# A step-by-step order written by hand: early products at steps of their own, a reordered front, and contexts divided two pairs at a time

## The chip, the cores and the metric

The kernel runs on one core of a Trainium2 chip. The metric is device microseconds for one execution, lower is better. TensorE (PE, with its weight loads as PEld) multiplies, VectorE (DVE), ScalarE (ACT) and GpSimd (POOL) do elementwise work, and SyncE (SP) starts most DMAs. Every engine runs its own instructions strictly in the order in which they were written for it, and semaphores order the engines among each other.

## The reference, cut to what matters

One transformer layer in float32 over x of 8 batches x 256 tokens x 256 features.

```
h = layernorm(x)
q, k, v = h @ Wq, h @ Wk, h @ Wv         # 32 query heads, 8 key heads, head size 8
q, k = rope(q), rope(k)
p = softmax(causal(q k^T / sqrt(8)))      # four query heads share a key head
x = x + layernorm((p v) @ Wo + b_out)
x = x + layernorm(moe(layernorm(x)))      # router top 2 of 8 experts, and 2 shared ones
```

The change touches only the attention part; the experts' part that follows is the same code.

## The kernel before

**The unit of work.** Attention is cut into 64 units, one for each batch and key head; unit k belongs to batch k // 8. A unit has four query heads of 256 tokens. For it the kernel needs the row maxima of the scores first, with queries along the partitions: `early(k)` makes the products of the first 128 tokens (one PSUM bank), `late(k)` those of the last 128 tokens (two neighbouring banks). On VectorE `tops(k)` (line 1069) takes the maxima of the first and `lates(k)` (line 1073) those of the second. After four units GpSimd makes three bf16 parts of the negated maxima (`neg`), TensorE turns them (`turn`), ScalarE copies them out (`turned`), and SP's DMA writes them into the query tile. `pass2(n)` makes the scores again, now with keys along the partitions and the maxima already subtracted, `exp` (line 922) takes the exponential, GpSimd zeroes what is not causal (line 1491), and `weigh(n)` multiplies with the values and a column of ones into bank 7, two units (a pair) side by side. `weighed` copies a pair's sums into `YC` (two buffers), `back` turns them to tokens along the partitions, and `divide` (lines 1082 and 1085) takes the reciprocal of the sums and multiplies the contexts into `CTX`, two buffers of one batch each. `b_turn`, `b_out` and so on carry a batch half (a tile of 128 tokens) through the output projection, layernorms and router.

**The order.** `plan()` writes one list of stages, and each engine walks it and takes its own stages. The list goes by steps n from -24. In step n the stages `early`, `tops`, `late`, `lates` of unit n + 7 stand beside `pass2(n)` and `exp(n)`; `weigh(n - 2)` follows. The string `ORDER` gives the order within a step; its s0 to s3 are quarter steps, at which the parts of the front (`FRONT0` for batch 0, `FRONT1` for batch 1, `FRONT` for the rest) and of the back (`BACK`) stand at slot 32 * batch + offset, and the second tile a lag later. In the front, `f_stats` and `f_dev` take a tile's statistics, `f_qkv` makes its products, `f_taken` (ScalarE) scales them out, `f_rope`, `f_first` to `f_fourth` (VectorE) and `k_first`, `k_third`, `k_twice` (ScalarE) turn them to rope and to three bf16 parts, and `q` and `k` are the DMA transposes on SP's queue into `QT` and `KT`. After the second tile's `k`, SP loads x of the batch two further on.

**Banks.** `banks()` gives each product of this part the least recently taken of PSUM banks 3 to 6. A product waits until the reader of the bank's last content has freed it: `divide` frees the bank of a `back`, `lates` that of a `late`, `b_low` that of a `b_turn2`, and so on.

**Idle products.** `WARM` lists how many products of a constant tile `mean` TensorE makes, with no reader, behind a stage, one number for each index: 12 ahead of the product that centres the weights (`mean`), 34 behind `f_qkv(3)`, and 14, 5, 4, 3, 3, 3, 3 behind `early(0)` to `early(6)`, 6 behind `late(0)`.

Of the kernel before, what the change touches and what calls it, by code (L numbers as in the profile page):

```python
# [5 lines left out]
F32 = mybir.dt.float32  # L6
# [3 lines left out]
ALU = mybir.AluOpType  # L10
# [3 lines left out]
P = 128  # L14
# [14 lines left out]
for k in range(NK):  # L29
# [6 lines left out]
EPS = 1e-5  # L36
LEAD = 7
START = -24
LAGS = (8, 12)
LAG = 16  # L40
EARLY = 55
SOON = 16
SHARED = 8
SPLIT = 6
WARM = {"mean": (12,), "f_qkv": (0, 0, 0, 34), "early": (14, 5, 4, 3, 3, 3, 3), "late": (6,)}
JOIN = 64
LAST4 = NT - 4
# [12 lines left out]


PICKS = ((0, 14), (14, 2))
# [62 lines left out]
def plan():  # L125

    out = []
    ahead = {}
    for n in range(64):
        ahead.setdefault(n - min(LEAD, LEAD + n // 2), []).append(n)  # L130
    halves, turns, turned, pairs, divided = [], [], [], [], []

    def sides(n):
        for b in range(NB):
            for stages, lag in (((FRONT0, FRONT1)[b] if b < 2 else FRONT, LAGS[b] if b < 2 else LAG), (BACK, 16)):
                for what, at in stages.items():
                    for T in range(2):
                        if n == max(32 * b + at + lag * T, 4 * START):
                            out.append((what, 2 * b + T))
                            if out[-1] == ("f_dev", 1):  # L140
                                out.append(("mean", 0))

    def step(n):
        firsts = ahead.get(n, [])
        for o in ORDER.split():
            if o == "2" and 0 <= n < 64:
                out.append(("pass2", n))
            if o == "x" and 0 <= n < 64:
                out.append(("exp", n))
            if o == "a":  # L150
                out.extend(("early", k) for k in firsts)
            if o == "d":
                out.extend(("tops", k) for k in firsts)
            if o == "b":
                out.extend(("late", k) for k in firsts)
            if o == "l":
                out.extend(("lates", k) for k in firsts)
            if o == "w" and 0 <= n - 2 < 64:
                out.append(("weigh", n - 2))
            if o == "W" and 0 <= n - 2 < 64 and n % 2:  # L160
                out.append(("weighed", (n - 2) // 2))
                pairs.append((n - 2) // 2)
            if o == "v":
                out.extend(("back", k) for k in pairs)
                divided.extend(pairs)
                pairs.clear()
            if o == "V":
                out.extend(("divide", k) for k in divided)
                divided.clear()
            if o == "m0":  # L170
                for k in firsts:
                    if k % 4 == 3:
                        out.append(("neg", k // 4, 0))
                        halves.append([k // 4, 1])
            if o in ("m1", "m2", "m3"):
                for h in halves[:1]:
                    if h[1] == int(o[1]):
                        out.append(("neg", h[0], h[1]))
                        h[1] += 1
                        if h[1] == 4:  # L180
                            turns.append(halves.pop(0)[0])
            if o == "t":
                out.extend(("turn", m) for m in turns)
                turned.extend(turns)
                turns.clear()
            if o == "T":
                out.extend(("turned", m) for m in turned)
                turned.clear()
            if o[0] == "s":
                sides(4 * n + int(o[1]))  # L190
# [10 lines left out]
    for c in range(NC + 4):  # L201
# [40 lines left out]
        if LAST + 4 <= c < LAST + 2 + NT:  # L242
            m = c - LAST - 2
# [71 lines left out]
def build(nc, x, xt, wqkv, wo, bout, wr, wsh, wa, wb, wc, rope, cf32, cbf, crf, out):  # L315
    ctx = ExitStack()
    with ctx:
# [3 lines left out]
        def sb(name, shape, dt, stack=ctx):  # L321
            return stack.enter_context(nc.sbuf_tensor(name, shape, dt))
# [3 lines left out]
        def bank(b, lo=0, hi=512):  # L326
            return PS[:, 512 * b + lo:512 * b + hi]
# [14 lines left out]
        identf = CF[:, 0:128]  # L342
# [11 lines left out]
        WRX = sb("WRX", [P, 2, 2, 8], F32R)  # L354

        behind = ExitStack()
        CTX = sb("CTX", [P, 2, 2, 256], F32, behind)
# [11 lines left out]
        sb("rest", [P, 320], F32)  # L369

        att = ExitStack()

        def ab(name, shape, dt):
            return sb(name, shape, dt, att)
# [5 lines left out]
        mean = ab("mean", [P, P], F32)  # L380
# [9 lines left out]
        RC = ab("RC", [P, 2, 8], F32)  # L390
# [7 lines left out]
        XTX = ab("XTX", [P, 2, 2, 2, 128], F32R)  # L398
        ident = CB[:, 0:128]
        corner = CB[:, 128:160]  # L400
        att.close()

        WH = [sb("WH0", [P, 3840], F32R)]
# [6 lines left out]
        early = ExitStack()  # L410
# [5 lines left out]
        late = ExitStack()  # L416
# [35 lines left out]
        full = [sem(f"full{b}") for b in range(8)]  # L452
        free = [sem(f"free{b}") for b in range(8)]
# [26 lines left out]
        right0, top0, laid, n_m, scored, expd, pv, sums, zeroed, ev = (sem(n) for n in ("right0", "top0", "laid", "n_m", "scored", "expd", "pv", "sums", "zeroed", "ev"))  # L480
# [4 lines left out]
        stages = plan()  # L485
# [63 lines left out]
        def _(eng):  # L549
            e = Waits(eng)  # L550
# [218 lines left out]
            for s in stages:  # L769
                what, i = s[0], s[1]  # L770
                if what == "mean":
# [3 lines left out]
                    c = take(s)  # L775
                    for k in range(2):
                        t = mm(bank(c, 0, 384), mean[:, :], WQ[:, k, :], k == 0, k == 1)
                    t.then_inc(full[c], 1)
                elif what == "f_qkv":
# [3 lines left out]
                    c = take(s)  # L783
# [17 lines left out]
                elif what == "turn":  # L801
                    e.wait_ge(n_3, i + 1)
                    c = take(s)
                    o = bank(c, 0, 128).bitcast(BF16)
# [5 lines left out]
                elif what == "weigh":  # L810
                    weigh(i)
                elif what == "back":
                    e.wait_ge(ev, i + 1)
                    e.wait_ge(d_cf, 16)
                    half_turn(s, YC[:, i % 2, :], identf)
                elif what == "b_turn":
                    for k in range(4):
                        read(e, ("back", 4 * (i // 2) + k))
                    half_turn(s, CTX[:, i // 2 % 2, i % 2, :], identf)
# [44 lines left out]
        def _(eng):  # L864
# [9 lines left out]
            for s in stages:  # L874
# [48 lines left out]
                elif what == "weighed":  # L923
                    h = i
                    e.wait_ge(pv, 2 * h + 2)
                    made(e, ("back", h - 2))
# [78 lines left out]
        def _(eng):  # L1005
# [68 lines left out]
                                      AXX, ALU.max, negate=True).then_inc(n_m, 1)  # L1074

            def divide(k):
                b, a = k // 4, k % 4
                c = use["back", k][0]
                src = bank(c, 0, 256).rearrange("p (t h x) -> p t h x", t=2, x=16)
# [632 lines left out]
```

## Time and profile before

| | us |
|---|---|
| median of three runs (657.97 to 658.33) | 658.25 |
| the profiled execution | 659.02 |
| its span, first to last instruction | 657.1 |

Read it so: the span is the part of an execution that the trace shows; 1.9 us lie around it. The first 45 us are the front before `exp(0)`, the steps of attention run from 45 to about 245 us, and from about 250 us on TensorE works on the experts' part. In the trace a product with float32 operands has two records, so that 12 idle products are 24 records.

### The profile page before, as it was taken

What the parts mean: (1) busy time and instruction counts of PE and PEld (TensorE: products, weight loads), DVE (VectorE), ACT (ScalarE), POOL (GpSimd) and SP (SyncE); (2) the same over time, 40 slices, a digit from 0 to 9 for tenths busy, and PEclk for the clock granted to TensorE, in tenths of its full rate; (3) what the DMA queues carried; (4) which work ended last, traced back from release to release, by engine and by line L of the source; (5) the groups of instructions that cost most, each with busy time, mean ns of one, the idle gap of its engine ahead of it and who ended that gap; (6) DMA issues with size and microseconds to landing.
All of it is one profiled execution on the core that took longest, in us unless ns stands there. A gap on an engine that the chain in (4) does not pass through costs nothing.

```text
span 657.1 us, 15356 instructions
## 1 busy us (share of the span) xinstructions
PE 631.5 (96%) x5934; PEld 518.5 (79%) x5934; DVE 531.3 (81%) x1055; ACT 423.2 (64%) x798; POOL 333.6 (51%) x528
## 2 busy tenths in 40 slices
PE   8997899999999979999999999999999999999995
PEld 6854456666655547888899999999999999888884
DVE  5699999999998744479879888888988888558886
ACT  2437788889887875542257876787877787422222
POOL 3227667877766761100275454545454530078864
PEclk9998999999999999999999999999999999999998
DMA  3953633655540000000367786877776864032311
GB/s 91 177 128 77 107 84 70 131 111 145 112 88 12 19 10 17 17 1 1 120 234 257 248 279 212 266 245 255 242 265 234 260 220 153 25 91 83 94 56 64
DMA packets 79671, 87.10 MB, mean 133 GB/s; under 512 B 54352, under 2 KB 69072, under 8 KB 79600
## 3 DMA queue, kind: packets, MB, share of 16 engines
q0 software_dynamic: 11872, 54.53, 25.1%
q1 hardware_dynamic: 67312, 31.08, 19.3%
q8 instruction: 47, 0.77, 0.5%
q10 hardware_dynamic: 416, 0.52, 0.3%
q14 instruction: 24, 0.20, 0.1%
HBM read 63.83 MB, written 9.31 MB: 111 GB/s over the span
## 4 chain that ended last, share of the span: by engine, by line
PE 79%; DVE 12%; issue 3%; ACT 3%; POOL 2%; SPq 1%; DMA 1%; POOLq 0%; DVEq 0%; ACTq 0%
PE PS L553 75%; DVE NM L1073 3%; DVE NM L1069 2%; PE PS L564 2%; PE PS L760 1%; ACT PF L922 1%; POOL PF L1491 1%; DVE X L1338 1%; DVE RR L1034 1%; PE PS L708 1%; DMA X<-in_x 1%; DVE RA L1027 1%; ACT WH L869 0%; POOL RS L1434 0%; SPq L1593 0%
## 5 line engine op out<-in xcount | busy, mean ns | idle before, releaser
L1278 DVE TENSOR_TENSOR HF<-SS,PS 128x256 f32<-128x256 f32 (+2 forms) x141 | 68.6, 487 | 66.7 <-ACT SS L968 37.9
L1357 DVE TENSOR_TENSOR WL<-RAW,WH 128x768 fp32r<-128x768 f32 x125 | 118.4, 958 | 4.4 <-ACT WH L869 4.1
L968 ACT ACTIVATE SS<-PS 128x256 f32<-128x256 f32 (+2 forms) x141 | 62.0, 440 | 79.2 <-PE PS L553 77.5
L869 ACT ACTIVATE HH<-HF 128x256 fp32r<-128x256 f32 (+1 forms) x120 | 58.0, 483 | 72.6 <-DVE HF L1278 70.3
L1491 POOL TENSOR_SCALAR_AFFINE_SELECT PF<-PF 128x512 f32<-128x512 f32 x128 | 83.1, 674 | 41.5 <-ACT PF L922 41.3
L869 ACT ACTIVATE WH<-RAW 128x768 fp32r<-128x768 f32 x125 | 103.3, 841 | 0.0
L553 PE MATMUL PS<-WH,HH 128*128 128x256 f32 x355 | 103.2, 291 | 0.2
L553 PE MATMUL PS<-WL,HH 128*128 128x256 f32 x355 | 100.3, 282 | 0.0
L553 PE MATMUL PS<-WH,HL 128*128 128x256 f32 x355 | 100.2, 282 | 0.0
L922 ACT ACTIVATE PF<-PS 128x1536 f32<-128x1536 f32 x64 | 92.8, 1449 | 11.4 <-PE PS L553 10.1
L553 PE MATMUL PS<-XGL,WH 128*128 128x256 f32 x320 | 90.5, 283 | 0.0
L553 PE MATMUL PS<-XGH,WH 128*128 128x256 f32 x320 | 90.3, 282 | 0.0
L553 PE MATMUL PS<-XGH,WL 128*128 128x256 f32 x320 | 90.3, 282 | 0.0
L1073 DVE TENSOR_REDUCE NM<-PS 128x4 f32<-128x1024 f32 x64 | 77.6, 1213 | 1.0 <-PE PS L553 0.9
L553 PEld LDWEIGHTS PS<-WH,HH 128*128 128x128 f32 x355 | 67.5, 190 | 2.7 <-ACT HH L869 0.3
L553 PEld LDWEIGHTS PS<-WL,HH 128*128 128x128 f32 x355 | 67.5, 190 | 2.0
L553 PEld LDWEIGHTS PS<-WH,HL 128*128 128x128 f32 x355 | 67.7, 191 | 0.0
L553 PE MATMUL PS<-XH,WH 128*128 128x512 f32 x160 | 64.1, 401 | 0.0
L1463 POOL DMA_INDIRECT RAW<-in_wa,WIDX x23 | 22.7, 985 | 80.5 <-DVE WIDX L1248 40.3
L553 PE MATMUL PS<-XL,WH 128*128 128x512 f32 x160 | 63.4, 396 | 0.0
L553 PE MATMUL PS<-XH,WL 128*128 128x512 f32 x160 | 63.1, 394 | 0.0
L1371 DVE TENSOR_TENSOR HL<-HF,HH 128x256 fp32r<-128x256 f32 (+1 forms) x120 | 62.3, 519 | 0.2 <-ACT HH L869 0.2
(212 smaller groups left out, 1488.3 us busy)
## 6 DMA issues: line engine op xcount, KB each, us to landing
ys<-YO SPq DMA_DIRECT2D x16, 256.0 KB, 3.1
RAW<-in_wsh SPq DMA_DIRECT2D x4, 768.0 KB, 4.6
XT<-in_xt SPq DMA_DIRECT2D x8, 256.0 KB, 3.3
X<-in_x SPq DMA_DIRECT2D x8, 256.0 KB, 3.3
xn<-YY SPq DMA_DIRECT2D x16, 128.0 KB, 1.7
out<-X SPq DMA_DIRECT2D x15, 128.0 KB, 1.7
ys<-YO SPq DMA_DIRECT2D x7, 128.0 KB, 2.3
RAW<-in_wsh SPq DMA_DIRECT2D x2, 384.0 KB, 5.1
```

What stands on the lines that cost most here:

```text
L553: return eng.matmul(o, l, r, start=start, stop=stop, skip_group_check=True)
L564: t = eng.transpose(bank(c, 128 * k, 128 * k + 128), src[:, 128 * k:128 * k + 128], idn)
L869: return eng.activation(o, i, ACT.Copy)
L922: eng.activation(PF[:, i % 3, :], PS[:, 0:1536], ACT.Exp, scale=SCALE).then_inc(expd, 1)
L968: eng.activation(ss, both(i, bank(b))[0], ACT.Silu).then_inc(free[b] if dense(i) else silu, 1)
L1069: eng.tensor_reduce(o, bank(c).rearrange("p (h t) -> p h t", t=128), AXX, ALU.max, negate=True).then_inc(free[c], 1)
L1073: eng.tensor_reduce(o.rearrange("p (j a) -> p a j", a=2), bank(c, 0, 1024).rearrange("p (a j t) -> p a j t", a=2, j=2), AXX, ALU.max, nega ...
L1278: eng.tensor_tensor(hf, ss, both(c, bank(b))[1], ALU.mult).then_inc(free[b], 1)
L1357: eng.tensor_tensor(WL[q % 2][:, c], RAW[raw_of(q)][:, c], WH[q % 2][:, c].bitcast(F32), ALU.subtract).then_inc(w_lo, 1)
L1371: eng.tensor_tensor(HL[:, i % 4, 0:n], HF[:, i % 2, 0:n], HH[:, i % 4, 0:n].bitcast(F32), ALU.subtract).then_inc(h_lo, 1)
L1463: eng.indirect_dma_start(RAW[raw_of(q)][:, 768 * lo:768 * hi], None, (wa, wb, wc)[k], bass.IndirectOffsetOnAxis(ap=WIDX[:, q - 1:q], axis= ...
L1491: eng.affine_select(out=o, in_=o, pattern=[[0, 4], [1, 128]], base=0, channel_multiplier=-1, compare_op=ALU.is_ge, fill=0.0).then_inc(zero ...
```

## The change

1. For the first seven units `early` and `tops` get steps of their own (`TOPS`), and `late` and `lates` others (`WHOLE`). Before, unit k stood with all four at step k - 7. Now `early` and `tops` of units 0 to 6 stand at -8, -7, -7, -5, -3, -2, -1, and `late` and `lates` at -8, -7, -6, -4, -3, -2, -1.
2. The slots of the front's parts change in all three tables, the second tile of batch 0 comes 9 slots behind the first and not 8, and `BACK`, `ORDER` and `WARM` change.
3. A `back` now turns two pairs, four transposes into one bank, every fourth step; `divide` takes one reciprocal of 32 and one product of 256 elements, where there were two of 16 and two of 128. `CTX` gets a third buffer, and lies elsewhere.

```diff
-LAGS = (8, 12)
+LAGS = (9, 12)
-WARM = {"mean": (12,), "f_qkv": (0, 0, 0, 34), "early": (14, 5, 4, 3, 3, 3, 3), "late": (6,)}
+WARM = {"mean": (16,), "f_qkv": (2, 0, 1, 24), "early": (4, 0, 4, 3, 2, 4, 0), "late": (0,)}
-FRONT = {"f_split": -88, "f_stats": -96, "f_dev": -93, "f_qkv": -78, "f_taken": -78, "f_rope": -74, "f_first": -69, "f_second": -67, "f_third":
-         -63, "q": -59, "k": -57, "k_first": -68, "k_third": -64, "f_fourth": -62, "k_twice": -61}
-FRONT0 = {"f_stats": -108, "f_dev": -111, "f_qkv": -87, "f_taken": -87, "f_rope": -83, "f_first": -81, "f_second": -80,
-          "f_third": -77, "q": -77, "k": -74, "k_first": -81, "k_third": -80, "f_fourth": -77, "k_twice": -73}
-FRONT1 = {"f_stats": -98, "f_dev": -95, "f_qkv": -77, "f_taken": -78, "f_rope": -78, "f_first": -78, "f_second": -71, "f_third":
-          -68, "q": -60, "k": -59, "k_first": -77, "k_third": -71, "f_fourth": -67, "k_twice": -66}
-BACK = {"b_turn": 46, "b_turned": 45, "b_out": 53, "b_taken": 54, "b_dev": 55, "b_add": 57, "b_stats2": 61, "b_dev2": 63,
-        "b_norm2": 66, "b_turn2": 70, "b_high": 69, "b_low": 68, "b_route": 75, "b_kept": 73}
-ORDER = "x a 2 b d l s1 s0 m0 s2 w m1 v t V m2 m3 s3 T W"
+FRONT = {"f_split": -87, "f_stats": -94, "f_dev": -89, "f_qkv": -78, "f_rope": -75, "f_taken": -77, "q": -56,
+         "f_first": -71, "f_second": -66, "k": -64, "k_first": -65, "f_third": -61, "k_third": -63, "f_fourth": -61,
+         "k_twice": -60}
+FRONT0 = {"f_stats": -131, "f_taken": -85, "f_dev": -112, "f_qkv": -91, "f_rope": -84, "f_first": -82, "q": -81,
+          "f_second": -77, "k_first": -79, "f_third": -77, "k_third": -78, "k": -79, "k_twice": -73, "f_fourth": -77}
+FRONT1 = {"f_dev": -105, "f_qkv": -79, "f_second": -70, "f_rope": -85, "f_first": -77, "f_taken": -86, "f_stats":
+          -110, "f_third": -68, "k_first": -72, "f_fourth": -65, "q": -62, "k": -51, "k_twice": -62, "k_third": -72}
+BACK = {"b_out": 52, "b_turned": 44, "b_dev": 53, "b_turn": 45, "b_add": 59, "b_taken": 54, "b_stats2": 62, "b_dev2":
+        63, "b_norm2": 67, "b_low": 68, "b_turn2": 70, "b_high": 70, "b_kept": 75, "b_route": 75}
+SHIFT = (0, 0, 0, 0, 0, 0, 0, 0)
+TOPS = (-8, -7, -7, -5, -3, -2, -1)
+WHOLE = (-8, -7, -6, -4, -3, -2, -1)
+ORDER = "a x d 2 l b s1 m0 s0 s2 m1 w t m2 v V m3 T s3 W"
...
-            if o == "v":
-                out.extend(("back", k) for k in pairs)
-                divided.extend(pairs)
+            if o == "v" and len(pairs) == 2:
+                out.append(("back", pairs[0] // 2))
+                divided.append(pairs[0] // 2)
                 pairs.clear()
...
-                    e.wait_ge(ev, i + 1)
+                    e.wait_ge(ev, 2 * i + 2)
                     e.wait_ge(d_cf, 16)
-                    half_turn(s, YC[:, i % 2, :], identf)
+                    c = take(s)
+                    for m in range(2):
+                        for T in range(2):
+                            at = 256 * T + 128 * m
+                            t = eng.transpose(bank(c, at, at + 128), YC[:, m, 128 * T:128 * T + 128], identf)
+                    t.then_inc(full[c], 1)
...
-                eng.reciprocal(RC[:, :, :], src[:, :, :, 8]).then_inc(sums, 1)
-                made(e, ("b_turn", 2 * b - 3))
+                eng.reciprocal(RC[:, :], src[:, :, 8]).then_inc(sums, 1)
+                made(e, ("b_turn", 2 * b - 5))
                 e.wait_ge(sums, k + 1)
-                eng.tensor_tensor(CTX[:, b % 2, :, 64 * a:64 * a + 64].rearrange("p t (h d) -> p t h d", d=8), src[:, :, :, 0:8],
-                                  RC[:, :, :].unsqueeze(3).broadcast_to([P, 2, 8, 8]), ALU.mult).then_inc(free[c], 1)
+                eng.tensor_tensor(CTX[:, b % 3, a, :, :].rearrange("p t (h d) -> p (t h) d", d=8), src[:, :, 0:8],
+                                  RC[:, :].unsqueeze(2).broadcast_to([P, 32, 8]), ALU.mult).then_inc(free[c], 1)
```

## Rows read from the trace of the kernel before

**Rows 1.** the page: busy time and share of the span of each engine.

```profile
PE 631.5 (96%) x5934; PEld 518.5 (79%) x5934; DVE 531.3 (81%) x1055; ACT 423.2 (64%) x798; POOL 333.6 (51%) x528
```

**Rows 2.** stretches: length; PE, PEld, DVE, ACT, POOL busy (count), clock, DMA share, GB/s.

```profile
40.00:60.00 20.00, 16.42 (x215) 9.30 (x212) 19.72 (x38) 13.53 (x21) 11.10 (x20) 0.91 0.42 107
...
143.24:156.11 12.87, 12.80 (x187) 8.03 (x186) 12.38 (x27) 11.45 (x21) 10.28 (x22) 1.00 0.69 176
...
181.86:194.43 12.57, 11.61 (x181) 7.03 (x179) 11.33 (x22) 10.68 (x19) 8.13 (x19) 1.00 0.32 67
...
250.00:300.00 50.00, 50.00 (x309) 43.23 (x308) 29.27 (x66) 24.86 (x46) 4.67 (x13) 1.00 0.03 9
```

**Rows 3.** the chain that ended last, first 30 us: start, length, what.

```profile
1.05 7.08 PE PS L553 x28
8.15 0.56 DVE WQ L1312
...
24.99 3.58 DMA X<-in_x
...
29.88 1.14 DVE NM L1073
```

**Rows 4.** timeline of the front: start, length, instruction, idle before and its releaser.

```profile
1.05 5.49 PE L553 MATMUL PS<-mean 128*128 128x128 f32 x24 [1.05 <-POOL mean L1418]
...
14.51 7.75 PE L553 MATMUL PS<-mean 128*128 128x128 f32 x68
...
18.20 0.51 ACT L869 ACTIVATE KC<-KC 128x384 bf16<-128x384 bf16 x1
...
18.73 1.24 SPq L1599 DMA_TRANSPOSE KT<-KC  x1
...
20.01 2.90 SPq L1593 DMA_TRANSPOSE QT<-QC  x1
...
23.30 3.39 PE L553 MATMUL PS<-mean 128*128 128x128 f32 x28
...
26.62 0.24 PE L553 MATMUL PS<-CB 32*32 32x64 bf16 x8
...
28.66 0.43 DVE L1315 BATCH_NORM_STATS2 BN<-X 128x6 f32<-128x256 f32 x1 [0.73 <-DMA X<-in_x]
...
36.02 1.56 PE L553 MATMUL PS<-WQ,XT 128*128 128x384 f32 x4
...
38.34 0.69 DVE L1069 TENSOR_REDUCE NM<-PS 128x4 f32<-128x512 f32 x1 [0.41 <-PE PS L553]
...
39.73 1.23 DVE L1073 TENSOR_REDUCE NM<-PS 128x4 f32<-128x1024 f32 x1 [0.69 <-PE PS L553]
```

**Rows 5.** VectorE groups with their forms, 45 to 100 us: count, busy, mean ns.

```profile
L1085 DVE TENSOR_TENSOR CTX<-PS,RC 128x128 f32<-128x128 f32 x6 | 1.7, 292 | 0.2
L1082 DVE RECIPROCAL RC<-PS 128x16 f32<-128x16 f32 x6 | 1.5, 244 | 0.2 <-PE PS L564 0.2
```

**Rows 6.** the same view, 100 to 200 us.

```profile
L1349 DVE TENSOR_TENSOR XL<-PS,XH 128x256 fp32r<-128x256 f32 x8 | 3.4, 425 | 2.4 <-ACT XH L869 2.3
```

**Rows 7.** the chain that ended last, 145 to 152 us.

```profile
145.67 0.18 DVE RC L1082
...
145.87 0.30 DVE CTX L1085
...
146.22 0.56 PE PS L553 x12
...
151.32 0.37 PE PS L564 x2
```

**Rows 8.** timeline of TensorE, one wait of the body's end.

```profile
191.28 0.28 PE L553 MATMUL PS<-B,ones 128*128 128x256 bf16 x1 [0.88 <-DVE CTX L1085]
```

**Rows 9.** one-microsecond stretches, columns as in the first table.

```profile
50.00:51.00 1.00, 0.26 (x9) 0.24 (x5) 1.00 (x3) 1.00 (x3) 0.58 (x2) 1.00 1.13 215
...
52.00:53.00 1.00, 1.00 (x12) 0.40 (x12) 0.95 (x3) 1.00 (x2) 1.00 (x3) 0.50 1.10 213
```

More of the change, by code:

```diff
@@ L127, in plan @@
     out = []
-    ahead = {}
+    tops, whole = {}, {}
     for n in range(64):
-        ahead.setdefault(n - min(LEAD, LEAD + n // 2), []).append(n)
+        tops.setdefault(TOPS[n] if n < LEAD else n - LEAD, []).append(n)
+        whole.setdefault(WHOLE[n] if n < LEAD else n - LEAD, []).append(n)
     halves, turns, turned, pairs, divided = [], [], [], [], []
@@ L134, in sides @@
         for b in range(NB):
-            for stages, lag in (((FRONT0, FRONT1)[b] if b < 2 else FRONT, LAGS[b] if b < 2 else LAG), (BACK, 16)):
+            front = (FRONT0, FRONT1)[b] if b < 2 else FRONT
+            for stages, lag, late in ((front, LAGS[b] if b < 2 else LAG, 0), (BACK, 16, SHIFT[b])):
                 for what, at in stages.items():
                     for T in range(2):
-                        if n == max(32 * b + at + lag * T, 4 * START):
+                        if n == max(32 * b + at + lag * T + late, 4 * START):
                             out.append((what, 2 * b + T))
@@ L143, in step @@
     def step(n):
-        firsts = ahead.get(n, [])
+        parts, firsts = tops.get(n, []), whole.get(n, [])
         for o in ORDER.split():
@@ L150, in step @@
             if o == "a":
-                out.extend(("early", k) for k in firsts)
+                out.extend(("early", k) for k in parts)
             if o == "d":
-                out.extend(("tops", k) for k in firsts)
+                out.extend(("tops", k) for k in parts)
             if o == "b":
@@ L356, in build @@
         behind = ExitStack()
-        CTX = sb("CTX", [P, 2, 2, 256], F32, behind)
         CTT = sb("CTT", [P, 2, 256], F32, behind)
@@ L368, in build @@
         RAW1 = sb("RAW1", [P, 3840], F32)
-        sb("rest", [P, 320], F32)
         att = ExitStack()
@@ L389, in build @@
         YC = ab("YC", [P, 2, 256], F32)
-        RC = ab("RC", [P, 2, 8], F32)
+        RC = ab("RC", [P, 32], F32)
         NMT = ab("NMT", [48, 2, 256], BF16)
@@ L400, in build @@
         corner = CB[:, 128:160]
+        CTX = ab("CTX", [P, 3, 2, 2, 128], F32)
         att.close()
@@ L812, in _ @@
                 elif what == "back":
-                    e.wait_ge(ev, i + 1)
+                    e.wait_ge(ev, 2 * i + 2)
                     e.wait_ge(d_cf, 16)
-                    half_turn(s, YC[:, i % 2, :], identf)
-                elif what == "b_turn":
-                    for k in range(4):
-                        read(e, ("back", 4 * (i // 2) + k))
-                    half_turn(s, CTX[:, i // 2 % 2, i % 2, :], identf)
+                    c = take(s)
[4 more added lines that the diff above has]
+                    t.then_inc(full[c], 1)
+                elif what == "b_turn":
+                    for k in range(2):
+                        read(e, ("back", 2 * (i // 2) + k))
+                    c = take(s)
+                    for k in range(2):
+                        t = eng.transpose(bank(c, 128 * k, 128 * k + 128), CTX[:, i // 2 % 3, k, i % 2, :], identf)
+                    t.then_inc(full[c], 1)
                 elif what == "b_out":
@@ L925, in _ @@
                     e.wait_ge(pv, 2 * h + 2)
-                    made(e, ("back", h - 2))
+                    made(e, ("back", h // 2 - 1))
                     copy(YC[:, h % 2, :], bank(7, 0, 256)).then_inc(ev, 1)
@@ L1076, in divide @@
             def divide(k):
-                b, a = k // 4, k % 4
+                b, a = k // 2, k % 2
                 c = use["back", k][0]
-                src = bank(c, 0, 256).rearrange("p (t h x) -> p t h x", t=2, x=16)
+                src = bank(c).rearrange("p (h x) -> p h x", x=16)
                 made(e, ("back", k))
                 read(e, ("back", k - 1))
-                eng.reciprocal(RC[:, :, :], src[:, :, :, 8]).then_inc(sums, 1)
-                made(e, ("b_turn", 2 * b - 3))
+                eng.reciprocal(RC[:, :], src[:, :, 8]).then_inc(sums, 1)
+                made(e, ("b_turn", 2 * b - 5))
                 e.wait_ge(sums, k + 1)
-                eng.tensor_tensor(CTX[:, b % 2, :, 64 * a:64 * a + 64].rearrange("p t (h d) -> p t h d", d=8), src[:, :, :, 0:8],
-                                  RC[:, :, :].unsqueeze(3).broadcast_to([P, 2, 8, 8]), ALU.mult).then_inc(free[c], 1)
+                eng.tensor_tensor(CTX[:, b % 3, a, :, :].rearrange("p t (h d) -> p (t h) d", d=8), src[:, :, 0:8],
+                                  RC[:, :].unsqueeze(2).broadcast_to([P, 32, 8]), ALU.mult).then_inc(free[c], 1)
             def prepare(k):
```

## The prediction

> **What bounds the kernel now.** I read the page first: TensorE is busy 96% of the span, VectorE 81% [rows 1]. That is a mean over stages with different limits, so the table of stretches comes next [rows 2]. From 250 us on TensorE is busy the whole stretch; the change leaves that part alone, and I take it that whatever attention ends earlier is kept to the end, one for one. From 40 to 60 us VectorE is busy 19.72 of 20 us and TensorE 16.42: here VectorE's work sets the pace. From 143 to 156 us, one turn of four steps (12.87 us), both are nearly full, TensorE with 12.80 and VectorE with 12.38 us, so a saving on one alone soon meets the other. From 182 to 194 us, at 12.57 us for four steps, TensorE is idle for 0.96 us. The front has a limit of its own, a chain of small steps [rows 3]: the products that centre the weights, the rope, transposes by DMA, and then, out of place, a wait for the load of x of batch 2, behind which the first maxima stand.
>
> **The change, part by part.** Times below are against the profiled execution, 659.02 us (span 657.1 and 1.9 around it); the median of the runs shown is 658.25, 0.77 less.
>
> *The start.* `mean` gets 16 idle products, not 12. The 12 (24 records) fill TensorE from 1.05 for 5.49 us, 0.23 us a record; later ones take 7.75 us for 68 records, 0.11 each [rows 4]. The product that centres the weights stands right behind them in the chain [rows 3]. Eight more records cost 0.9 to 1.8 us; a part comes back where the four real products behind them run faster. I take a loss of 0.7 (0.2 to 1.8).
>
> *To the first maxima.* In batch 0, `f_taken(1)` now stands behind `k_third(0)`, which delays the second tile by about 0.8 with the loss above, and `k_twice(0)` stands ahead of `k_first(1)`. It now begins at 18.20, and SP's transpose of the first keys at 18.73 [rows 4]; the copy could run over a microsecond earlier, so SP can go on when its first transpose of Q is out. The second tile's transpose of Q, at 20.01, comes 0.8 us later, the one of K behind it 0 to 0.8 later, and so the loads of x that follow it on SP. `late(0)` needs that K: its products at 26.62 stay between 26.2 and 27.5.
>
> On VectorE, `f_stats(4)` waits 0.73 us for x and starts at 28.66, and only then come `tops(0)` and `lates(0)` at 29.88 [rows 3, 4]. The work ahead of that wait ended at 27.93. In the new order `f_stats(4)` stands behind `lates(0)`, and the parts of batch 1 ahead of the maxima are interleaved so that one tile's `f_rope` fills the wait for ScalarE's copies of the other. I put the maxima of `late(0)` at 27.5 to 28.5, 1.4 to 2.4 us earlier. The statistics (0.6) then fall behind them and may meet the wait for x, whose load (3.58 us from issue) starts up to 0.8 later than 24.99: it lands at 28.6 to 29.4. What is left when both are done is 0.6 to 1.9; I take 1.3.
>
> *Steps -7 to 0.* VectorE waits for TensorE ahead of `tops(4)` 0.41 us and ahead of `lates(4)` 0.69 us, since `f_qkv(4)` (1.56 us) and three idle products stand ahead of `late(4)` [rows 4]. With units 1 and 2 made ahead, other work of VectorE covers `late(2)` and `late(3)`, and `early(4)` has two idle products and not three: 0.4 of these 1.1 us goes. The front as a whole gives 1.3 + 0.4 = 1.7 (0 to 2.5; the 0.7 at the start is in it already, as everything above is counted from the later start).
>
> *Contexts.* Dividing a pair costs 0.292 + 0.244 us of VectorE [rows 5]. No row shows a reciprocal of 32 or this product of 256 elements. For the product the nearest is a subtraction of 256 elements from PSUM, 0.425 us [rows 6]; against 0.292 for 128 that is 0.16 us for the instruction and 1.04 ns an element, which makes a reciprocal of 32 take 0.26. Two pairs cost 0.69 and not 1.07: 0.38 us saved (nothing, if the strided form took twice the time an element; 0.54, if an instruction's length did not matter). From 45 to 100 us, where VectorE sets the pace, six divisions become three: 3 x 0.38 = 1.1 (0 to 1.6).
>
> *The body, to 182 us.* Here I followed which product takes which bank. In step 4j + 3 before, `late` takes the bank of the `back` of the step before, so that it waits for `divide`; that wait is in the chain: reciprocal, product, then TensorE at 146.22 [rows 7]. Without it TensorE could have begun about 0.15 us earlier. With a `back` every fourth step the same `late` takes banks of `lates` and `b_kept`, which are free by then. Of TensorE's own time, two pairs in one `back` save a wait and an issue: a `back` stands in the chain for 0.37 us [rows 7], 0.74 for two; the second pair's two transposes behind the first's I put at 0.22, 0.59 together. That is 0.15 + 0.15 = 0.3 a turn, less 0.05 for a new wait (below), over 6 turns 1.5 (0 to 3; the upper end is TensorE's and VectorE's idle time of a turn, 0.07 + 0.49).
>
> *182 to 220 us.* There TensorE waits 0.88 us, for a bank that a `divide` frees, ahead of `b_out` [rows 8]. In the new order `b_out` takes the bank that `f_taken` freed. I take 0.8 of the 0.96 idle us [rows 2], and for the next two turns 0.3: 1.1 (0 to 1.3). After 220 us ScalarE and GpSimd make the chain; nothing of that changes.
>
> *Edits put at nothing.* `k_twice` goes a quarter step back and SP's `k` one step forward, ahead of `q`: SP now stands at `k` until `k_twice` is done, and behind it wait a store of `b_norm2`, the copy of `turned` and then `q`. All of these are needed two or more steps, over 6 us, later. `b_dev` moves ahead of `f_rope` on GpSimd and holds it until `b_taken` is done; behind it waits the copy of the values, needed a batch later, and the next causal mask, for which there is slack as long as `b_taken` ends before the next `exp`. In every second turn `b_taken` (about 1 us of ScalarE) now stands ahead of `b_high`, for which `b_low` and, through its bank, `late` wait. `f_rope` (about 1 us) stands ahead of `b_low` on VectorE and hides that but for 0.1 to 0.3 us in two turns; `b_low` waits 2.3 us in eight already today [rows 6]. The third `CTX` buffer takes a wait away that was never last.
>
> Sum: 1.7 + 1.1 + 1.5 + 1.1 = 5.4 us, 653.6 against 659.02, and 652.9 against the median.
>
> **The clock, weighed.** TensorE's granted clock fell to 0.50 (1.2 GHz) at 51 us, behind a stretch in which it was busy 0.26 of 1 us [rows 9]; from 23 to 31 us idle products kept it full, 3.39 us of them alone between `early(0)` and `late(0)` [rows 4]. The new order has 4 there and not 14, so TensorE stands still for some 2.5 us. The Trainium skill (TensorE: Matmul & The Clock Gate, on HAM oscillation) says that idle gaps between bursts of matmuls throttle the array again and that the next burst starts at half rate; by that rule the front's gain is mostly lost, which is the first rival below. That clock fell in this trace without a full stop, so the trace leans to the rule.
>
> **The rivals.** *Front at half clock.* `late(0)` to `late(3)` and `f_qkv(4)` run at 1.2 GHz: 1.56 us becomes some 3, and a little at each `late`; 1.5 to 2 us are lost: 654.7. For it speaks the fall at 51 us, against it that VectorE's work covers most products there.
>
> *The body is TensorE's alone.* If the four transposes take as long as two pairs do now and the wait for `divide` is filled by another, 1.5 + 0.3 fall away: 654.7 too, up to 655.4 with a smaller gain at 190.
>
> *All of it and more.* Both engines' idle time in a turn goes, the front reaches its bound: 2.5 + 1.5 + 3 + 1.3 = 8.3: 650.
>
> *Slower.* Half clock in the stretch from 45 to 100 us. TensorE has gaps there (16.42 busy of 20) and the few idle products no longer fill up to it; with the shifted order the falls could repeat. In the turn at full clock TensorE's work is 12.80 us, 3.2 a step, the same as VectorE's pace; at half clock most of it takes 1.6 times that, so a step loses about 1.9 us. The forecast's 5.4 us are gone after three such steps, some 15 us at half clock where now there are 3.4; with 20 us the time is 661.
>
> *No change.* Front lost to half clock and no gain in the body: 657 to 659.
>
> **How the numbers follow.** The forecast, 652.9, has 0.46; its own range is 651 to 654.5. Front at half clock 0.16, body TensorE's alone 0.13, all and more 0.10, no change 0.05, slower 0.10. Faster by over 0.2% (1.3 us, about what can be told from no change here) is the first four, 0.85; within it 0.05; slower 0.10. The range of 648.5 to 657.5 takes in the first four with their bounds and leaves out the last two.
>
> **What would show it.** Right: `tops(0)` starts near 27 and `f_stats(4)` behind the first `lates`; `exp(0)` about 1.7 us earlier than 45.0; the exponentials of the body have a turn of about 12.6 us and not 12.87; `divide` is 16 times a reciprocal near 0.26 and a product near 0.43; no wait of TensorE for CTX. Wrong: the clock at 0.50 before 45 us or for more than a few us in all up to 100; a turn of 12.8 or more; waits of TensorE for `b_low` or `turned`; the start of the weights' centring later by over 1 us.

## The result, and the profile after

The changed kernel took 667.07 us (median of 5 runs, 665.28 to 670.88) against 658.25 for the kernel before in runs beside it (657.6 to 658.87). The ratio is 1.0149, with a 95% interval of 1.0115 to 1.0183: slower by 8.8 us, where 652.9 was forecast, and outside the range. Its profiled execution took 665.95 us with a span of 664.2, 7.1 more than the span before. Medians are of all runs of a kernel; the ratios are estimated from the single runs, without those in the slow state (two of six in experiment 1, 695.86 and 706.65 us), and so differ a little from the quotient of two medians.

The page's first row, to be read against [rows 1]:

```profile
PE 628.2 (95%) x5880; PEld 514.4 (77%) x5880; DVE 535.0 (81%) x1023; ACT 422.8 (64%) x798; POOL 332.5 (50%) x528
```

VectorE has 32 instructions fewer, and 3.7 us more work. That row says where to look, but not when. For that I read the starts of the 64 exponentials on ScalarE in both traces; they cut the span into stretches that can be compared one by one (in all tables of this kind: profiled execution, us).

| stretch | before | after | change |
|---|---|---|---|
| start to exponential 0 | 44.98 | 43.83 | -1.15 |
| 0 to 16 | 52.01 | 55.51 | +3.50 |
| 16 to 32 | 51.95 | 52.79 | +0.84 |
| 32 to 36 | 12.87 | 17.12 | +4.25 |
| 36 to 63 | 80.36 | 79.87 | -0.49 |
| 63 to the end | 414.93 | 415.08 | +0.15 |

The parts add to 7.10. Two places hold the loss: the first sixteen steps, and one hole between 32 and 36. The rest of the kernel was kept one for one, as assumed.

**The hole.** The chain that ended last, of the changed kernel, start, length, what:

```profile
143.84 0.42 ACT KC L882
...
144.28 1.23 SPq L1612
...
149.47 0.43 SPq L1598
...
149.95 8.08 DMA QT<-QC
...
158.07 2.38 PE PS L558 x17
```

SP's own timeline there:

```profile
144.28 1.23 SPq L1612 DMA_TRANSPOSE KT<-KC  x1
145.56 0.58 SPq L1576 DMA_DIRECT2D XT<-in_xt  x1
146.19 1.19 SPq L1572 DMA_DIRECT2D X<-in_x  x1
147.44 0.45 SPq L1636 DMA_DIRECT2D xn<-YY  x1
147.94 1.49 SPq L1621 DMA_DIRECT2D QT<-NMT  x2
149.47 0.43 SPq L1598 DMA_DIRECT2D RAW<-in_wsh  x1
149.95 4.38 SPq L1606 DMA_TRANSPOSE QT<-QC  x1
```

and TensorE's, with its wait in brackets:

```profile
158.07 0.24 PE L558 MATMUL PS<-CB 32*32 32x64 bf16 x8 [2.53 <-DMA QT<-QC]
```

ScalarE ends the copy of the keys (`k_twice`) at 144.26; only then can SP issue `k`, and behind it, in its queue, stand two loads, a store, two copies of maxima and the first load of the shared experts' weights (768 KB). `q` comes last, 5.7 us after `k`, holds SP for 4.38 us and lands 8.08 us after it was issued, 13.8 us behind the issue of `k`. TensorE wanted it at 155.5, 11.3 us behind the issue of `k`. In the trace of before SP issued the same `q` ahead of `k`:

```profile
139.16 1.92 SPq L1593 DMA_TRANSPOSE QT<-QC  x1
141.12 1.77 SPq L1599 DMA_TRANSPOSE KT<-KC  x1
```

**The clock.** Stretches of the changed kernel, columns as in [rows 2]:

```profile
24.00:26.00 2.00, 0.17 (x9) 0.10 (x8) 1.38 (x4) 0.98 (x3) 0.00 (x0) 0.93 0.94 205
52.00:54.00 2.00, 0.28 (x12) 0.11 (x10) 2.00 (x4) 1.57 (x2) 2.00 (x4) 1.00 0.18 42
56.00:58.00 2.00, 0.12 (x2) 0.00 (x0) 2.00 (x3) 1.50 (x2) 1.91 (x4) 1.00 0.41 76
59.60:63.00 3.40, 3.40 (x41) 1.64 (x41) 3.33 (x9) 0.89 (x2) 0.88 (x3) 0.54 0.03 7
71.00:73.00 2.00, 0.07 (x8) 0.07 (x8) 2.00 (x4) 1.42 (x2) 0.64 (x2) 1.00 0.93 73
73.30:76.70 3.40, 3.40 (x26) 2.34 (x22) 3.21 (x7) 1.46 (x3) 1.26 (x3) 0.53 0.57 115
```

Behind the stops at 24, 56 and 71 us, and behind the hole, the granted clock fell to half, 1.2 GHz: for 6.8 us from 25.7 on, and for 3.4 us each from 59.8 (the rows' 0.54 and 0.53 have an edge in them), 73.5 and 158.8. Behind the stop at 52 us it did not fall; it stayed full until 59.8. The kernel before had one such spell ahead of its last microseconds, 3.4 us long [rows 9]. In the three stops from 52 to 73 us VectorE is busy throughout, and TensorE's waits of 1.72, 2.06 and 1.97 us there end with VectorE's maxima: TensorE stands because VectorE is late.

**VectorE.** Its groups with their forms, 100 to 155 us after, count | busy, mean ns:

```profile
L1067 DVE TENSOR_TENSOR QC<-RT,QC 128x256 bf16<-128x256 f32 x5 | 4.1, 824 | 0.0
L1041 DVE TENSOR_TENSOR RB<-RQ,ROPE 128x160 f32<-128x160 f32 x4 | 3.0, 748 | 0.0
L1351 DVE SCALAR_TENSOR_TENSOR X<-YY,RS,X 128x256 f32<-128x256 f32 x4 | 2.8, 706 | 0.0
L1047 DVE TENSOR_TENSOR RR<-RA,RB 128x320 f32<-128x320 f32 x4 | 2.5, 630 | 0.0
...
L1098 DVE TENSOR_TENSOR CTX<-PS,RC 128x256 f32<-128x256 f32 x4 | 1.7, 424 | 0.1
...
L1095 DVE RECIPROCAL RC<-PS 128x32 f32<-128x32 f32 x4 | 1.4, 357 | 0.1
```

and of before, 100 to 152 us, the same work:

```profile
L1338 DVE SCALAR_TENSOR_TENSOR X<-YY,RS,X 128x256 f32<-128x256 f32 x4 | 2.3, 587 | 0.0
...
L1054 DVE TENSOR_TENSOR QC<-RT,QC 128x256 bf16<-128x256 f32 x4 | 2.0, 506 | 0.0
...
L1034 DVE TENSOR_TENSOR RR<-RA,RB 128x320 f32<-128x320 f32 x4 | 1.9, 481 | 0.0
...
L1028 DVE TENSOR_TENSOR RB<-RQ,ROPE 128x160 f32<-128x160 f32 x4 | 1.4, 348 | 0.0
```

The same instructions on the same tiles take longer: 0.32 + 0.40 + 0.12 + 0.15 = 0.99 us a turn, against 0.29 us that the division by two pairs saves. (Others became shorter by 0.17 in all, the remainder of the keys from 312 to 225 ns above all, so that VectorE's busy time rose from 12.45 to 13.00 us a turn between exponentials 16 and 32.) What the four have in common is that both tensors they read lie in SBUF; the product that reads PSUM takes the forecast 424 ns throughout, and the maxima (from PSUM too) are at 1212 and 1213 ns. The same happens at one of the places where TensorE stands. VectorE's timeline after:

```profile
69.91 0.65 DVE L1124 CAST WRX<-WRF 128x16 fp32r<-128x16 f32 x1
70.59 0.55 DVE L1126 TENSOR_TENSOR WRX<-WRF,WRX 128x16 fp32r<-128x16 f32 x1
71.07 0.68 DVE L1082 TENSOR_REDUCE NM<-PS 128x4 f32<-128x512 f32 x1
```

GpSimd's at the same time:

```profile
68.77 0.97 POOL L1520 TENSOR_TENSOR XTX<-XT,XTX 128x256 fp32r<-128x256 f32 x1
69.89 1.23 POOL L1504 TENSOR_SCALAR_AFFINE_SELECT PF<-PF 128x512 f32<-128x512 f32 x2 [0.16 <-ACT PF L935]
```

VectorE's before:

```profile
70.41 0.17 DVE L1111 CAST WRX<-WRF 128x16 fp32r<-128x16 f32 x1
70.62 0.17 DVE L1113 TENSOR_TENSOR WRX<-WRF,WRX 128x16 fp32r<-128x16 f32 x1
70.71 0.68 DVE L1069 TENSOR_REDUCE NM<-PS 128x4 f32<-128x512 f32 x1
```

and GpSimd's before:

```profile
70.78 1.23 POOL L1491 TENSOR_SCALAR_AFFINE_SELECT PF<-PF 128x512 f32<-128x512 f32 x2 [1.24 <-ACT PF L922]
```

Two instructions on 16 columns take 0.17 us each before, when GpSimd's causal mask begins behind them, and 0.65 and 0.55 when it runs beside them. TensorE's next products wait for the maxima behind them: 0.93 us before, 1.97 after. By the Trainium skill (SBUF — State Buffer, in "SBUF: two separate sides") VectorE and GpSimd share one pair of ports as an exclusive lock, held for a whole instruction, which an instruction of VectorE takes if it has two SBUF inputs or runs in a two-port mode. The rows agree as far as two inputs go, 748 against 348 ns on one tile, and 424 as forecast where one input is in PSUM. The cast of 16 columns has one input and was longer too (0.65 against 0.17); whether it ran in such a mode no run here shows.

### The profile page after: what moved, and what is told of

The parts are those of the page before. It is cut to its first block, busy times and chain, and to the rows that moved or that the text cites. A ratio compares the mean times of both kernels' runs of the same rounds, so it can differ in the third digit from the quotient of the medians.

```text
span 664.2 us, 15193 instructions
## 1 busy us (share of the span) xinstructions
PE 628.2 (95%) x5880; PEld 514.4 (77%) x5880; DVE 535.0 (81%) x1023; ACT 422.8 (64%) x798; POOL 332.5 (50%) x528
## 4 chain that ended last, share of the span: by engine, by line
PE 74%; DVE 14%; ACT 4%; issue 2%; DMA 2%; POOL 2%; SPq 1%; POOLq 0%; DVEq 0%; ACTq 0%
PE PS L558 70%; DVE NM L1086 5%; DVE NM L1082 2%; ACT PF L935 2%; DMA QT<-QC 2%; PE PS L765 1%; DVE RR L1047 1%; PE PS L824 1%; POOL PF L1504 1%; DVE RB L1041 1%; DVE RA L1040 1%; PE PS L713 1%; SPq L1612 1%; ACT QC L882 1%; DVE QC L1067 0%
## 5 line engine op out<-in xcount | busy, mean ns | idle before, releaser
L1086 DVE TENSOR_REDUCE NM<-PS 128x4 f32<-128x1024 f32 x64 | 77.6, 1213 | 4.8 <-PE PS L558 4.8
L558 PE MATMUL PS<-KT,QT 64*128 64x256 bf16 (+1 forms) x512 | 62.2, 252 | 0.4
```

The costliest lines, as they stand in the source:

```text
L558: return eng.matmul(o, l, r, start=start, stop=stop, skip_group_check=True)
L1086: eng.tensor_reduce(o.rearrange("p (j a) -> p a j", a=2), bank(c, 0, 1024).rearrange("p (a j t) -> p a j t", a=2, j=2), AXX, ALU.max, nega ...
```

## The experiments

The first four ran on a chip where the kernel before took 660.27 us (658.94 to 665.95), the last four on one where it took 658.26 (657.14 to 658.67). Ratios are to the kernel before on the same chip. Where two ratios of different chips are compared, each kernel was measured against the kernel before beside it, not against the other.

**1. `q` back to its old place.** The changed kernel with one number changed:

```
-FRONT = {... "q": -56, ...}
+FRONT = {... "q": -59, ...}
```

> The changed kernel with one number put back: in FRONT, q at -59 and not at -56, so that SP issues the transpose of Q ahead of the copy of the maxima and, for batches 5 to 7, ahead of the shared experts' weights (768 KB). Theory A (the transpose of Q waits in the DMA queue behind those weights, TensorE stands still for it once, and the clock falls behind that): the landing 8.1 us after the issue at 150 us becomes 4 to 5, the wait of TensorE on QT<-QC (2.7 us) and the half clock behind it are gone, the exponential 34 comes 4 us earlier, the median falls from 667.1 to about 662.5. Rival (the step was late for another reason, TensorE or VectorE were behind): the wait moves to another releaser and the time stays within 1 us of 667.

689.64 us, ratio 1.0399 (1.034 to 1.0459): far slower, a miss. `q` now stood ahead of the copies of the maxima but still behind `k`, which waits for `k_twice` (48.1 us of SP's time from 100 to 200 us, nearly as in the changed kernel, 48.7); now those copies, with `q` and its 1.5 to 3.9 us on SP ahead of them, were late. The waits, 100 to 200 us (total, times, longest):

```profile
PEld PS L558 <- DMA QT<-NMT: 12.8, 7, 3.7
```

A turn took 14.9 us on average from exponential 20 to 44. The kernel before also had `q` and `k` ahead of these copies, but no wait for `k_twice` in front of them. So I put the trouble not to `q` alone but to a queue in which `k`, with its wait, stands ahead of everything that is due sooner; `k` alone at its old place was not tried.

**2. The idle products of before.** The changed kernel with

```
-WARM = {"mean": (16,), "f_qkv": (2, 0, 1, 24), "early": (4, 0, 4, 3, 2, 4, 0), "late": (0,)}
+WARM = {"mean": (12,), "f_qkv": (0, 0, 0, 34), "early": (14, 5, 4, 3, 3, 3, 3), "late": (6,)}
```

> The changed kernel with the idle products of the kernel before (WARM put back). Theory A (half clock in the front and from 55 to 80 us comes from the few idle products): no half clock before 45 us, exp(0) at about 43 and not 43.8, one spell at most from 45 to 80 us, 665 or less. Rival (the idle products do not matter for the rest: the falls from 45 us on come from TensorE's own gaps, where neither kernel has idle products): the spells from 50 us on stay, the time is within 1.5 us of the changed kernel's 667.1, and may be worse in the front, since the idle products stand ahead of real ones.

667.39 us, ratio 1.0092 (1.0062 to 1.0122), 0.6% better than the changed kernel's 1.0149, by intervals that overlap a little and on another chip. There was one half-clock spell of 3.4 us up to 90 us in place of three of 13.6 in all, yet the first sixteen steps took 55.53 us, as long as in the changed kernel (55.51). What became shorter was the hole, 14.33 us against 17.12 from exponential 32 to 36; exponential 0 came 1.5 us later, where 43 us was expected for it. The transpose of `q` took 7.60 us to land here too, but TensorE waited 1.58 us for it and not 2.53, and no fall of the clock followed: so not all of the 4.25 us is the wait, part is the half clock behind it. And from 16 to 32 the four turns took 51.61 us, less than in the kernel before (51.95), although VectorE's instructions were as long as in the changed kernel. So fewer falls of the clock alone don't bring the loss of the first sixteen steps back, in the one trace of this kernel.

**3. Contexts alone.** The kernel before with the division by two pairs and the third `CTX` buffer, nothing else:

```
-            if o == "v":
-                out.extend(("back", k) for k in pairs)
+            if o == "v" and len(pairs) == 2:
+                out.append(("back", pairs[0] // 2))
...
```

> The kernel before with one part of the change: contexts divided by two pairs and the third buffer; all slots, steps, idle products and the order string are those of before. Theory A (this part is good by itself: 0.29 us of VectorE less for two pairs, measured 0.357 + 0.424 against 1.07, and no wait of TensorE for a bank that a division frees): 1 to 3 us faster than before, 655.5 to 657, a turn of 12.6 to 12.8 us. Rival (the turn is TensorE's alone, or the division of two pairs blocks VectorE longer at the wrong place): within 0.7 us of 658.25, turn 12.87.

665.46 us, ratio 1.0064 (1.0034 to 1.0094): slower by itself, where 1 to 3 us less were expected. VectorE's groups, 100 to 155 us:

```profile
L1350 DVE SCALAR_TENSOR_TENSOR X<-YY,RS,X 128x256 f32<-128x256 f32 x4 | 3.3, 824 | 0.0
L1040 DVE TENSOR_TENSOR RB<-RQ,ROPE 128x160 f32<-128x160 f32 x4 | 3.0, 752 | 0.0
```

Nothing but the lump of the division was moved (and `CTX` got its third buffer), and the `b_add` product went from 587 to 824 ns and the first rope product from 348 to 752: 0.64 us a turn, for 0.29 saved.

**4. Steps of the early maxima alone.** The kernel before with the two lists of steps:

```
+TOPS = (-8, -7, -7, -5, -3, -2, -1)
+WHOLE = (-8, -7, -6, -4, -3, -2, -1)
...
```

> The kernel before with one part of the change: the early products and maxima of the first seven units at steps of their own (TOPS, WHOLE); all else is of before, idle products too. Theory A (this takes VectorE's wait for x out from ahead of the first maxima): the first maxima at 27 to 28 and not 29.2, exp(0) 1 to 1.5 us earlier, 657. Rival (the other work stands behind them and the gain is lost by step 0, or the idle products, bound to the units' numbers, now delay the late products): within 0.7 us of 658.25 or slower.

662.28 us, ratio 1.0016 (0.999 to 1.0043): no difference that can be told; the gain of 1 to 1.5 us ahead of exponential 0 did not come (45.12 us).

**5 and 6. The causal mask cut.** Both kernels with the mask on 4 of the 128 columns of a head; the rest of the masking is left out.

```
...
-pattern=[[0, 4], [1, 128]], base=0
+pattern=[[0, 4], [1, 4]], base=0
...
```

> The changed kernel with GpSimd's causal mask cut to 4 of its 128 columns a head (the rest of the mask is left out; same instructions, order and semaphores). Theory B (VectorE's operations that read two SBUF tiles run slower while GpSimd's mask runs, and the new order puts more of them beside it: rope's second product 0.75, the bf16 remainder 0.78, the sum 0.62, the residual 0.67 to 0.70 us, where before they took 0.35, 0.51, 0.48, 0.59): all four go back to the durations of before or below, and the turn falls from 12.85 to 12.3 or less. Rival (they are slower for their own operands or the DMA traffic): the durations stay and the turn with them.

> The kernel before with the same cut of the causal mask to 4 of 128 columns. Theory B (in the order of before few of VectorE's operations meet the mask): the durations of VectorE's operations hardly change, and the turn stays at 12.6 to 12.87, set by TensorE; the changed kernel with the same cut then has a turn 0.2 to 0.5 shorter. Rival (the mask itself, which stands ahead of weigh, is on the path of both): both turns fall by the same.

After: 663.68 us (1.0086, 1.0064 to 1.0107). Before: 653.42 (0.993, 0.9913 to 0.9947). Two runs each. The durations fell back at once. VectorE in the changed kernel with the cut mask, 100 to 155 us:

```profile
L1047 DVE TENSOR_TENSOR RR<-RA,RB 128x320 f32<-128x320 f32 x4 | 1.9, 482 | 0.0
L1351 DVE SCALAR_TENSOR_TENSOR X<-YY,RS,X 128x256 f32<-128x256 f32 x4 | 1.9, 474 | 0.0
...
L1067 DVE TENSOR_TENSOR QC<-RT,QC 128x256 bf16<-128x256 f32 x4 | 1.6, 407 | 0.0
...
L1041 DVE TENSOR_TENSOR RB<-RQ,ROPE 128x160 f32<-128x160 f32 x4 | 1.3, 318 | 0.0
```

So the mask beside them is what lengthened them. In the kernel before some became shorter too (the `b_add` product from 587 to 476 ns). The totals can't be set side by side: this execution of the changed kernel had a half clock of 30.7 us from 24 us on, and its exponential 0 came 6.9 us later than in the kernel before with the same cut. The stretches below can.

The turn was a miss in both. Four turns from exponential 16 on took 51.98 us in the changed kernel, 13.00 each and not 12.3 or less, and 51.54 in the kernel before, so the changed one was longer still and not shorter by 0.2 to 0.5 a turn:

```profile
101.36:153.34 51.98, 50.54 (x748) 32.29 (x744) 47.15 (x99) 45.56 (x86) 26.15 (x84) 1.00 0.51 97
127.10 0.13 PEld L558 LDWEIGHTS PS<-QT,KT 64*128 64x128 bf16 x2 [1.54 <-DMA QT<-NMT]
```

VectorE now has 4.83 us to spare, and in one place SP's queue ends last: at 127.10 TensorE has waited 1.54 us for a copy of maxima, which SP issued at 123.92, 4.92 us behind `k` and behind two loads and a store. That one wait is more than the 0.44 us by which the stretch is longer than in the kernel before.

**7. The weights behind `q`.** The changed kernel with the three loads of the shared experts' weights issued behind `q(11)` to `q(13)`, and not behind the copies of `turned(8)` to `turned(10)`:

```
-                    if SHARED <= i < SHARED + 3:
-                        shared(0, 0, i - SHARED)
...
+                    if SHARED + 3 <= i < SHARED + 6:
+                        shared(0, 0, i - SHARED - 3)
```

> The changed kernel with the loads of the shared experts' weights issued on SP behind the transposes of Q of the steps 30, 34 and 38, and not behind the copies of the maxima, one step ahead of these transposes. Nothing else moves. Theory A (the transpose of Q of batch 5 waits behind 768 KB of weights in the DMA queue): landing 4 to 5 us after its issue, no wait on QT<-QC near 155 us, no half clock near 159 us, 4 us faster than the changed kernel. Rival (the transpose is late because SP issues it late, behind k and the copies): the wait stays.

662.63 us, ratio 1.0075 (1.0046 to 1.0105), half of the loss. SP's timeline:

```profile
152.16 1.70 SPq L1606 DMA_TRANSPOSE QT<-QC  x1
153.90 1.22 SPq L1598 DMA_DIRECT2D RAW<-in_wsh  x1
```

`q` still comes 5.9 us behind `k`, which was issued at 146.28, but it holds SP for 1.70 us and not 4.38, lands after 4.28 and not 8.08, and the hole is gone: 13.11 us from exponential 32 to 36, not 17.12.

**8. The kernel before again**, one execution.

> The kernel before, unchanged, once more on this chip, to have its trace beside the others: how far the front (exp(0) at 44.98), the turn (12.85) and the stretch behind the last exponential (414.9 us) move by themselves. Expected: within 0.5, 0.03 and 3 us.

657.26 us. Exponential 0 moved by more than the 0.5 us expected, the rest by less than expected. By stretches:

| kernel | to 0 | 0 to 16 | 16 to 32 | 32 to 36 | 36 to 63 | end |
|---|---|---|---|---|---|---|
| before | 44.98 | 52.01 | 51.95 | 12.87 | 80.36 | 414.93 |
| before again (8) | 43.39 | 51.99 | 51.95 | 12.87 | 80.36 | 414.94 |
| before, mask cut (6) | 43.40 | 50.30 | 51.54 | 12.76 | 78.91 | 414.39 |
| steps of maxima (4) | 45.12 | 53.05 | 51.92 | 12.87 | 80.30 | 416.54 |
| contexts (3) | 43.66 | 53.33 | 52.57 | 13.07 | 81.49 | 418.38 |
| after | 43.83 | 55.51 | 52.79 | 17.12 | 79.87 | 415.08 |
| after, mask cut (5) | 50.31 | 51.05 | 51.98 | 13.41 | 79.43 | 414.22 |
| idle products (2) | 45.32 | 55.53 | 51.61 | 14.33 | 79.85 | 416.96 |
| weights behind q (7) | 43.16 | 58.60 | 52.56 | 13.11 | 79.75 | 415.02 |
| q back (1) | 43.64 | 63.63 | 61.60 | 14.51 | 84.56 | 417.36 |

On the first chip (1 to 4) the part behind exponential 63 is longer by 1.6 to 3.4 us in every kernel, so their totals are compared with the kernel before there. The table carries most of what follows. Between two executions of the kernel before only the front moved, by 1.59 us. From exponential 0 to 32 the changed kernel lost 4.34 us against before; with the mask cut in both 1.19 (51.05 + 51.98 against 50.30 + 51.54), although its clock stayed at half until 54 us. The cut mask also frees GpSimd itself, so that this 3.15 us is what the new order pays for running beside GpSimd, its longer instructions and whatever waited for the mask. Most of it lies in the first sixteen steps (3.50 us of loss against 0.75 with the cut); from 16 to 32 it is 0.84 against 0.44.

## Why the prediction was wrong

Two steps failed. *Edits put at nothing* is the first. It said of SP that it "now stands at `k` until `k_twice` is done", listed what waits behind, and dismissed it: all of it "needed two or more steps, over 6 us, later". It left out that the queue behind `k` is itself 5.7 us long, that a 768 KB load is in it three times, and that a transpose right behind such a load took 8.08 us to land the first time and 7.55 the second (TensorE did not wait for that one, nor for the third, 5.02). It cost 4.25 us in one place, the wait and the half clock behind it; with the load moved the stretch took 4.0 less (experiment 7). The margin was there in the forecast's own words, over 6 us, and was never set against the sum of the queue: 5.7 + 8.1 = 13.8 us, where TensorE wanted `q` after 11.3. Experiment 1 shows how thin it is on the other side, and with the mask cut the copies of the maxima were late behind `k` by 1.54 us.

*Contexts* and *the body*. The product was right, 424 ns against 425. The reciprocal of 32 takes 357 ns, not 0.26 us, since I put its element at a multiplication's price: 16 more cost 113 ns, 7 ns each. Two pairs cost 0.78, 0.29 saved and not 0.38. (Of its bounds the lower was a slip: with twice the time an element its own prices still save about 0.1 and not nothing.) The four transposes of a `back` were right in size, 0.59, and so was the end of TensorE's wait for `divide`: it is gone. But the turn did not become 12.6, it is 13.20 from exponential 16 to 32 (52.79 / 4), where before it is 12.99. This is the second step that failed, and it is the same for both: durations were taken as fixed when instructions were moved. VectorE gained 0.29 us a turn and lost 0.99 in the four instructions beside the mask. It became the engine that ends last. Over the four turns from exponential 16, before and after:

```profile
96.99:148.93 51.94, 51.29 (x750) 32.21 (x745) 49.81 (x106) 45.83 (x85) 40.88 (x84) 1.00 0.49 107
99.34:152.13 52.79, 50.94 (x746) 32.24 (x748) 51.98 (x99) 45.84 (x85) 40.30 (x84) 1.00 0.54 90
```

TensorE's own work fell by 0.35 us, but its idle time rose from 0.65 to 1.85; VectorE's fell from 2.13 to 0.81, and the chain that ended last, from 100 to 119 us, is VectorE's. That VectorE's lengths alone do not fix the turn is shown by experiment 2 (12.90 with the same lengths), and the cut mask (13.00) shows that the 0.3 forecast on TensorE did not come without them either. Not every turn is VectorE's: the first row below answers to the second of [rows 2] (13.11 us for four steps, of which TensorE is busy for 12.98).

```profile
126.17:139.28 13.11, 12.98 (x197) 8.24 (x197) 12.53 (x22) 11.37 (x21) 10.10 (x21) 1.00 0.51 74
189.00:201.41 12.41, 11.99 (x190) 7.30 (x191) 11.35 (x21) 10.73 (x20) 8.52 (x19) 1.00 0.43 80
```

*182 to 220 us.* Its mechanism was right. The second of these rows answers to the third of [rows 2]: TensorE's idle time fell from 0.96 to 0.42 us; from exponential 36 to 63 the gain is 0.49 us of 1.1 forecast, and experiments 2 and 7 have 79.85 and 79.75 there.

*The front.* The four idle products ahead of the centring cost 0.05 us, not 0.7: their eight records took 0.33 more, the four real products behind them 0.32 less, and VectorE went on at 8.20 and not 8.15 (in experiment 7, the same program up to there, at 7.58: this start moves by itself). The first early maxima came 3.6 us sooner, the first late ones at 26.83, better than the 27.5 to 28.5 forecast. Then half the clock took most of it back, as the first rival had it:

```profile
28.69 2.08 PE L558 MATMUL PS<-mean 128*128 128x128 f32 x8
...
30.69 0.29 PE L558 MATMUL PS<-CB 32*32 32x64 bf16 x8
...
31.59 1.23 DVE L1086 TENSOR_REDUCE NM<-PS 128x4 f32<-128x1024 f32 x1 [1.21 <-PE PS L558]
```

Eight records of idle products took 2.08 us (1.16 at full clock at 22.94), and the next late maxima began at 31.59 against 31.99 before. Exponential 0 came 1.15 us earlier than in one execution of before and 0.44 later than in the other: no gain of the front can be told from the kernel's own spread.

*The clock.* The rival "slower" named the right stretch and sign and had 0.10; its price was too high. It charged 0.36 us for each us at half clock (by which 20 us make about 660, not 661). Experiment 7 is the same program as the changed kernel up to 149 us, and its execution had 20.4 us of half clock between 44 and 90 us where the other had 6.8: 3.09 us longer from 0 to 16 for 13.6 us more, 0.23 each, an estimate from two executions. And the one spell of before (3.4 us) cost nothing: the execution without it took 51.99 us, with it 52.01. The rule of the Trainium skill that was weighed in the prediction (TensorE: Matmul & The Clock Gate, on HAM oscillation) held in part: behind four of the changed kernel's five stops TensorE worked at 1.2 GHz. Behind the one at 52 us it did not, nor in the second execution of the kernel before, where TensorE was busy for 0.56 of 2.30 us from 51.80 on and the clock stayed full. And in experiment 7 it fell at 44.9, behind 3 us in which TensorE was busy for 2.15. The falls were not most of the loss: with the idle products of before the changed kernel had a single spell of 3.4 us up to 90 us, and still 55.53 us from 0 to 16. That the stops themselves were, because VectorE was late, is what the cut mask speaks for (3.50 us of loss there became 0.75).

What stays open: how the other 5 us (experiment 7) divide between the new order of batches 0 and 1 and that of the later ones. There is no result for the front alone, for the body alone, or for the moved weights together with the old idle products. Of the 3.5 us from 0 to 16 the contexts alone made 1.3 (experiment 3) and the maxima's steps 1.0 (experiment 4); that these add is an assumption. No version faster than the kernel before was found among those that compute the whole reference.

## What to carry to other kernels

When an instruction with a wait is moved ahead in a queue, add up everything queued behind it, issue times and landing times, and set that sum against the moment when its last member is due; a step that is due "over 6 us later" is not covered if the queue is 5.7 us long and its last member takes 4.3 us to land, 8.1 behind a big load. Two engines that share something make durations depend on the order: if VectorE is within a few per cent of full, a saving of 0.3 us a turn has to be checked against what will now lie beside GpSimd's instructions. And cut the span at a landmark that both traces have: behind the front, stretches of the kernel before repeated to 0.02 us between executions whose totals differed by 1.8.

## What the runs showed of the hardware

- A transpose by DMA (128 x 2048, bf16) issued 0.48 us behind a load of 768 KB on the same queue held SP for 4.38 us and landed 8.08 us from issue (in experiment 2, 4.22 and 7.60); with the load behind it, 1.70 us on SP and 4.28. Two loads of 256 KB and a store of 128 KB just ahead did much the same to SP, 3.87 us, but less to the landing, 5.90 (experiment 1).
- VectorE's reciprocal from PSUM: 244 ns for 16 columns, 345 to 358 for 32, so 6 to 7 ns a column, where a product from PSUM goes from 291 to 424 ns for 128 more, 1.0 each.
- Instructions of VectorE on 16 columns took 0.17 us alone and 0.55 to 0.65 beside GpSimd's mask of 128 x 512; on 256 columns 407 to 474 ns with the mask cut, up to 824 with it.
- The order with more and longer stops of TensorE is also less steady: from exponential 0 to 16 the changed kernel took 55.51 us and, in experiment 7, the same instructions 58.60, the kernel before 52.01 and 51.99. The changed kernel's five runs spread over 5.6 us, those of the kernel before over 1.3.
